# Post-norm attention and mixture block: held values, projections on odd slots, sums read outside the norm

## Reference

```python
qkv = (x @ w_qkv).reshape(B, S, 3, H, D)
q, k, v = (qkv[:, :, 0], qkv[:, :, 1], qkv[:, :, 2])
q = _unit_norm(q)          # t * rsqrt(sum(t * t) + EPS)
k = _unit_norm(k)
q = m * _apply_rope(q, cos, sin) + (1.0 - m) * q      # every second head is rotated
k = m * _apply_rope(k, cos, sin) + (1.0 - m) * k
logits = jnp.einsum('bshd,bthd->bhst', q, k) * q_gain[None, :, None, None]
logits = jnp.where(causal[None, None], logits, jnp.finfo(logits.dtype).min)
attn = jax.nn.softmax(logits, axis=-1)
y = jnp.einsum('bhst,bthd->bshd', attn, v).reshape(B, S, Dm)
```

## Time and profile before

| | us |
|---|---|
| median of 3 runs | 1081.23 |
| lowest and highest run | 1080.83, 1082.02 |
| span of the profiled execution | 1101.7 |
| TensorE busy in it | 1056.5 |
| VectorE, ScalarE, GpSimd busy in it | 623.5, 543.4, 395.7 |

### The profile page before, as it was taken

How to read it: one execution, slowest core, us unless ns; L and a number is a source line. 1 busy time by engine, 2 the same in 40 slices (tenths; PEclk the granted TensorE clock), 3 DMA queues, 4 the chain that set the end, 5 groups by cost and what they waited for, 6 DMA issues and landing times.

```text
span 1101.7 us, 17977 instructions
## 1 busy us (share of the span) xinstructions
PE 1056.5 (96%) x6171; PEld 753.5 (68%) x6172; DVE 623.5 (57%) x1094; ACT 543.4 (49%) x900; POOL 395.7 (36%) x323
## 2 busy tenths in 40 slices
PE   7799999999999999999999996899999999999996
PEld 6654656645566466643477674589999999998885
DVE  3578694896848777687688452232222222223776
ACT  3467776687767776778645410123222222221213
POOL 2232132321224222214342177082466664623430
PEclk9999999999999999999999998799999999999999
DMA  6444514463353624346163036253444443423443
GB/s 192 131 130 136 160 63 125 129 173 96 97 143 106 182 58 116 106 129 177 48 207 110 7 147 239 88 194 103 155 155 155 131 155 102 134 85 105 125 134 115
DMA packets 106097, 141.58 MB, mean 129 GB/s; under 512 B 12784, under 2 KB 57328, under 8 KB 106032
## 3 DMA queue, kind: packets, MB, share of 16 engines
q1 hardware_dynamic: 89664, 103.22, 31.9%
q10 hardware_dynamic: 11088, 20.19, 5.3%
q0 software_dynamic: 5280, 17.31, 4.8%
HBM read 84.59 MB, written 56.10 MB: 128 GB/s over the span
## 4 chain that ended last, share of the span: by engine, by line
PE 83%; ACT 6%; DVE 5%; issue 3%; POOL 1%; another core or an unknown queue 1%; DMA 0%; SPq 0%; ACTq 0%; DVEq 0%
PE scores L630 14%; PE scores L1495 12%; PE bank L1445 12%; PE bank L1545 9%; PE scores L704 7%; PE bank L618 7%; PE bank L751 6%; ACT probs L1647 4%; PE scores L529 4%; PE bank L1542 3%; PE scores L646 2%; DVE key_sum L1768 1%; PE scores L595 1%; PE bank L1474 1%; POOL wqkv_l L1845 1%
## 5 line engine op out<-in xcount | busy, mean ns | idle before, releaser
L1647 ACT ACTIVATE probs<-scores,shift_now 128x1024 f32<-128x1024 f32 (+3 forms) x296 | 273.6, 975 | 82.4 <-PE scores L1495 64.5
L1768 DVE TENSOR_TENSOR key_sum<-key_sum,probs 128x2048 f32<-128x2048 f32 (+1 forms) x96 | 204.1, 2126 | 53.8 <-PE bank L1545 18.8
L1495 PEld LDWEIGHTS scores<-q_stack,k_stack 96*128 96x128 f32 x640 | 104.6, 190 | 137.9 <-ACT probs L1647 71.5
L1495 PE MATMUL scores<-q_stack,k_stack 96*128 96x512 f32 (+3 forms) x640 | 188.4, 405 | 3.7 <-ACT probs L1647 3.4
L1545 PE MATMUL bank<-probs,v_sb 128*32 128x512 f32 (+3 forms) x1184 | 136.7, 534 | 0.0
L630 PE MATMUL scores<-ffn_w,xt_h 128*128 (+1 forms) x608 | 127.4, 331 | 0.0
L1217 POOL TENSOR_TENSOR ffn_w<-raw,ones 128x1408 fp32r<-128x1408 f32 (+4 forms) x36 | 72.1, 2013 | 134.1 <-PE bank L618 97.0
L630 PEld LDWEIGHTS scores<-ffn_w,xt_h 128*128 128x128 f32 x608 | 99.8, 189 | 7.7 <-issue 5.5
L704 PE MATMUL scores<-x1T_h,ffn_w 128*128 128x512 f32 x352 | 92.2, 396 | 9.2 <-DVE silu L1043 6.4
L1009 DVE TENSOR_TENSOR ht_l<-scores,ht_h 128x256 fp32r<-128x256 f32 x39 | 16.6, 425 | 145.8 <-ACT ht_h L833 145.8
L1524 POOL TENSOR_SCALAR_AFFINE_SELECT probs<-probs 128x512 f32<-128x512 f32 x40 | 43.0, 1077 | 151.4 <-ACT probs L1647 151.2
(11 more groups left out here) (243 smaller groups left out, 1726.8 us busy)
## 6 DMA issues: line engine op xcount, KB each, us to landing
q_stack<-turn_scratch SPq DMA_DIRECT2D x48, 256.0 KB, 3.9
k_stack<-turn_scratch SPq DMA_DIRECT2D x48, 256.0 KB, 4.2
x_sorted<-zeros SPq DMA_DIRECT2D x39, 256.0 KB, 2.9
y_sorted<-y_tile ACTq DMA_DIRECT2D x39, 256.0 KB, 2.6
x_tile<-x_sorted ACTq DMA_DIRECT2D x37, 256.0 KB, 2.7
turn_scratch<-turned_h SPq DMA_DIRECT2D x32, 256.0 KB, 2.0
turn_scratch<-turned_l SPq DMA_DIRECT2D x32, 256.0 KB, 2.0
raw<-w_gate SPq DMA_DIRECT2D x8, 704.0 KB, 5.5
```

Of the source, the lines that this page charges most:

```text
L1495: mm = nc.tensor.matmul(scores[:, p, hh, lo:CH], k_stack[0:3 * HD, h, j * P:(j + 1) * P], q_stack[0:3 * HD, i % 2, h, lo:CH], start=True, ...
L1647: nc.scalar.activation(exponents(g, slot)[:, 2 * p:2 * p + 2, lo:CH], scores[:, p, :, lo:CH], ACT.Exp, bias=shift_now[:, p:p + 1]).then_in ...
L1768: nc.vector.tensor_tensor(key_sum[:, :, lo:CH], key_sum[:, :, lo:CH], probs[:, slot % 4, :, lo:CH], ALU.add).then_inc(sum_dve, 1)
```

## The change

Three edits:

- Held slots. `held(g, slot)` is true for an odd slot with a projection. There TensorE skips the values at the slot's end; in the next slot it does, after scores, projection and turn, the values of both.
- The tables: most projections move to odd slots, and norms, rotations, turns and stacks with them. For chunk 0 the projections go from slots 25 to 28 of the group before to 27, 28, 29 and 31, the norm from 28 to 31, the rotation from 29 to 32, the turns from 32 and 35 to 35 and 36. For chunk 1 the projections go from 31, 33, 36, 37 to 33, 35, 36, 37, norm and rotation each a slot later. For chunk 2 only the norm goes from 4 to 5. For chunk 3 the projections go from 8 to 11 to 7, 9, 11 and 13, the norm from 11 to 13, the rotation from 13 (14 in group 0) to 15, the turn of q from 16 to 17.
- The sums of step 1 are read in `dve_outputs` as those of all other steps, no longer inside the norm.

```diff
-SUMS_INSIDE = 11
-PROJECT_AT = {(0, 0): -15, (0, 1): -14, (0, 2): -13, (0, 3): -12, (1, 0): -9, (1, 1): -7, (1, 2): -4, (1, 3): -3,
-              (2, 0): 1, (2, 1): 2, (2, 2): 3, (2, 3): 5, (3, 0): 8, (3, 1): 9, (3, 2): 10, (3, 3): 11}
-NORMALISE_AT = {(0, 0): -12, (1, 0): -4, (2, 0): 4, (3, 0): 11}
...
+PROJECT_AT = {(0, 0): -13, (0, 1): -12, (0, 2): -11, (0, 3): -9, (1, 0): -7, (1, 1): -5, (1, 2): -4, (1, 3): -3,
+              (2, 0): 1, (2, 1): 2, (2, 2): 3, (2, 3): 5, (3, 0): 7, (3, 1): 9, (3, 2): 11, (3, 3): 13}
+NORMALISE_AT = {(0, 0): -9, (1, 0): -3, (2, 0): 5, (3, 0): 13}
...
+def held(g, slot):
+
+    return slot % 2 == 1 and any(True for _ in work_at(PROJECT, slot, g))
...
+                    if held(g, slot):
+                        continue
+                    if slot and held(g, slot - 1):
+                        pe_values(g, slot - 2)
                     if slot or later(g):
                         pe_values(g if slot else g - 1, (slot - 1) % SLOTS)
...
-        def dve_rsqrt(out, work, arg, ready, steps, inside=None):
+        def dve_rsqrt(out, work, arg, ready, steps):
...
-                if inside and turn == 1:
-                    inside()
...
         def dve_outputs(g, i):
             step = NC * g + i
-            if STEP_AT[i + 1] != SUMS_INSIDE + 1:
-                dve_read_sums(g, i)
+            dve_read_sums(g, i)
```

More of the change, by code:

```diff
@@ L53 @@
 STEP_AT = [0, 4, 12, 24, 40]
-SUMS_INSIDE = 11
 SLOTS = STEP_AT[-1]
-PROJECT_AT = {(0, 0): -15, (0, 1): -14, (0, 2): -13, (0, 3): -12, (1, 0): -9, (1, 1): -7, (1, 2): -4, (1, 3): -3,
-              (2, 0): 1, (2, 1): 2, (2, 2): 3, (2, 3): 5, (3, 0): 8, (3, 1): 9, (3, 2): 10, (3, 3): 11}
-NORMALISE_AT = {(0, 0): -12, (1, 0): -4, (2, 0): 4, (3, 0): 11}
[L62 to L71, removed]
+PROJECT_AT = {(0, 0): -13, (0, 1): -12, (0, 2): -11, (0, 3): -9, (1, 0): -7, (1, 1): -5, (1, 2): -4, (1, 3): -3,
+              (2, 0): 1, (2, 1): 2, (2, 2): 3, (2, 3): 5, (3, 0): 7, (3, 1): 9, (3, 2): 11, (3, 3): 13}
+NORMALISE_AT = {(0, 0): -9, (1, 0): -3, (2, 0): 5, (3, 0): 13}
+ROTATE_AT = {(0, 0): -8, (1, 0): -2, (2, 0): 6, (3, 0): 15}
+TURN_AT = {(0, 0): -5, (0, 1): -4, (1, 0): 1, (1, 1): 3, (2, 0): 8, (2, 1): 13, (3, 0): 17, (3, 1): 23}
+STACK_AT = {(0, 0): -4, (0, 1): -2, (1, 0): 2, (1, 1): 4, (2, 0): 10, (2, 1): 15, (3, 0): 18, (3, 1): 31}
+PROJECT_FIRST = {(3, 0): 7, (3, 1): 9, (3, 2): 11, (3, 3): 13}
+NORMALISE_FIRST = {(2, 0): 2, (3, 0): 13}
+ROTATE_FIRST = {(2, 0): 6, (3, 0): 15}
+TURN_FIRST = {(1, 1): 0, (2, 0): 8, (2, 1): 13, (3, 0): 17, (3, 1): 24}
+STACK_FIRST = {(1, 0): 2, (1, 1): 4, (2, 0): 10, (2, 1): 14, (3, 0): 18, (3, 1): 28}
 LOAD_W_AT = 18
@@ L1713, in dve_rsqrt, with dve_norms @@
                 n += 3
-        def dve_norms(g, c, inside=None):
+        def dve_norms(g, c):
             C = NC * g + c
@@ L1724, in dve_norms @@
                 nc.vector.wait_ge(normed, C)
-            dve_rsqrt(inv_norm[:], newton[:], sq_sum[:], norm_steps, 13 * C + 2, inside)
+            dve_rsqrt(inv_norm[:], newton[:], sq_sum[:], norm_steps, 13 * C + 2)
             nc.vector.tensor_tensor(inv_norm[:, 0], inv_norm[:, 0],
@@ L1833, in group @@
                     for gg, c, _ in work_at(NORMALISE, slot, g):
-                        dve_norms(gg, c, (lambda: dve_read_sums(g, 1)) if slot == SUMS_INSIDE else None)
+                        dve_norms(gg, c)
                     if slot == SPLIT_W_AT and has_following(g):
```

## The result

The changed kernel takes 1112.53 us, median of 4 runs (1111.49 to 1117.58), against 1081.62 for the kernel before beside it (4 runs): a ratio of 1.029, 95% interval 1.026 to 1.031. It is slower by 31 us, where 8.6 were forecast, and outside the range.

A forecast was written before the change was run, and what follows sets the result against it. The prediction took TensorE to bound the kernel, almost without gaps in the attention. Gains of 14.6 and 0.9 us against waits of 15.4, 6.3 and 2.4 gave +8.6 on 1081.2: 1089.8 us, range 1074 to 1099.

The forecast's parts named there:

- the three waits that it priced: TensorE waiting for the mask of slot 33 (5.1 us), the turn in slot 17 (2.1) and the turn in slot 8 (0.8).
- the sum: All gains and waits added: -14.6 - 0.9 + 15.4 + 6.3 + 2.4 = +8.6 us, giving 1089.8 us.
- paid in full: Any wait that the change puts in front of a TensorE instruction costs its whole length.
- the stacks: Scores waiting for q_stack and k_stack by SyncE's DMAs: taken as 0, bound 5.6 us at seven places.
- Part 1: Held values on TensorE: cheaper borders between matmuls save 0.34 us in each of 43 held slots, 14.6 us.
- Part 2: Projections moved: slot 25 loses its projection and a 0.31 us wait for wqkv_l; three transitions gain 0.9 us.
- Part 3: Values of slot 33 wait for GpSimd's mask behind its later rotation: 5.1 us a transition, 15.4 us in three.
- Part 4: Turn in slot 17 waits 2.1 us for chunk 3's rotation, 6.3 us in three groups; moving the sums' reading costs nothing.
- Part 5: Turn of chunk 2 in slot 8 waits 0.8 us for the rotated q in groups 1 to 3: 2.4 us.
- stacks or masks later: Rival: 0.8 us at seven places or a mask of 2.58 us, 5.6 to 5.8 more, 1095.5 us; chance 0.12.

The follow-up runs named there:

- e_fill: The changed kernel with 22 matmuls of 512 columns into an unused bank ahead of the values of slot 33, groups 0 to 2: 1122.08 us, ratio 1.030.

## Why the prediction was wrong

It was right on the sign, on the places of the three waits that it priced and on what ends them, and wrong on the size: 31 us in place of 8.6. The step that failed is the sum. It took "paid in full" to mean a wait's length and nothing behind it, where the runs show 10.6 us more by TensorE's clock; it took 0 for the stacks, where they show 5.8; and it had no term for late sums and additions, where they show 2.5. By its own steps, measured from slot 3:

- Part 1, 43 x 0.34 = 14.6: each border is as priced where nothing waits. But "a held slot is worth 0.34" holds only where the next slot asks nothing new. Where the next slot projects too, TensorE waits for ScalarE's copy; the prediction took 0 for that, and pairs of this kind save 0.07 to 0.10. Held on the old tables gave 2.8 for 26 slots, held on the new ones 5.9 net of the waits that it lengthened.
- Part 2, weights: 0.9 forecast; that wait of 0.8 no longer stands in the view of waits.
- Part 3, mask of slot 33: forecast 5.1 a transition, measured 5.5, 16.5 in all (slot 34 takes 8.92 us at full clock in e_fill, 3.4 of them work). GpSimd was as late as forecast (12.56 us against 12.54), TensorE was earlier: from the end of projection 31 its work took 7.69 us, not 8.05. The prediction priced the scores of 33 as a full block, 1.03, but they have 384 columns and take 0.81, and the scores of 34, which stand behind a projection, at 1.13 in place of 1.02.
- Part 4, turn in slot 17: forecast 2.1, measured 2.2 (slot 17 of 5.65 us at full clock, less 3.42), 6.7 in all.
- Part 5, turn in slot 8: forecast 0.8 in three groups, measured 1.0 (4.00 less 2.98) in two, 2.0 in all. In group 3 slot 8 takes 2.88 and no such wait stands there; TensorE had waited for k_stack in slot 7. Stacks: forecast 0, bound 5.6, measured 5.8 us of waits by DMA. The prediction had said that slot 4 comes earlier after its turn; most of the wait is at slot 12, and it did not ask when q_stack lands there.
- What no part had: TensorE's clock after a standstill. In slots 34 and 35 it cost 5.7 us over three groups. In slots 17 and 18 it cost another 4.9 (slot 17 took 7.05, 7.19 and 7.28 against 5.65 in e_fill, where that slot ran at full clock in two groups; slot 18 took 2.36, 2.22 and 2.12 against 2.12). 10.6 us in all.
- What no part had either: 1.0 by an addition and 1.5 by sums read, and 1.4 at the starts of the groups, whose cause stays open.

So for the stretch from slot 3: waits 16.5 + 6.7 + 2.0 + 5.8 + 2.5 + 1.4 = 34.9, clock 10.6, together 45.5; less 0.8 us for the weights 44.7 (short waits for exponents fell by 0.4 and those for other masks rose by as much). Measured are 31.9, so 12.8 us are left as what holding saved, where 14.6 were forecast. That is a remainder and no measurement: the view's gap of 5.35 us stands for a loss of 5.5, and if the ten or so other short gaps understate theirs by as much, holding comes to some 14. Either way 20.3 of the 23.3 us between forecast and measurement (31.9 less 8.6) are terms that were put at nothing; each of the priced ones is off by less than 2.

The rival "stacks or masks later" had the stacks. The trace of before had a hint of the clock: its profiled execution has low clock in the expert stage, where TensorE stood (waits of 6.40 and 4.20 us at 681 and 692 us), and the prediction read 20.5 us of difference between span and median without asking where they came from.

In slot 34 the granted clock was 0.50 from 436 to 442 us, behind a wait of 5.35. The Trainium skill (TensorE: Matmul & The Clock Gate, "HAM oscillation — how this bites in real kernels") tells of a kernel whose groups of matmuls each wait for a transfer and so each start at the low clock. The trace agrees, with a wait for GpSimd in place of a transfer.

## What to carry to other kernels

When TensorE is the bound and a change puts a standstill of some microseconds in front of it, price it in two parts, the wait and the work behind it at half the clock; here the second was 0.2 to 0.4 of a wait of 5.5 us and, where it came at all, 0.7 of one of 2.2. When steps are moved later in a table, list for each moved step what is queued behind it on its own engine (here a mask behind a rotation, a stack behind a load, exponents behind a copy), since each of the large losses was an innocent instruction behind a moved one. Grouping work of one tiling together is worth its 0.3 us a time, but pick the places where the next slot asks for nothing: 20 well chosen held slots gave 4.2 us, 26 gave 2.8. And when one profiled execution stands for a kernel, look for stretches of work that the edit does not touch and take them out of the comparison.
